# A vision transformer tower on one core: router logits four images side by side, two images loaded and scaled at the end of attention, and another order of the work in the output projection

## The reference, cut to what matters

```python
# layer 0, router: x1 is [8*1030, 192], 16 experts, each takes its capacity of best rows
scores = sigmoid(x1 @ gate_weight.T)
topk_score, topk_ids = top_k(scores.T, capacity)            # capacity 1030
out = (silu(xg @ Wg) * (xg @ Wu)) @ Wd * topk_score         # then added to its rows, and a shared expert
# layer 1, attention over 12 heads of 16; then
h3 = h2 + merge(heads) @ Wo + bo                            # the output projection
x3 = norm(h3)                                               # what router and experts of layer 1 take
logits = x3 @ w_router.T                                    # 8 experts, top 2 of each row
shared = (silu(x3 @ sg.T) * (x3 @ su.T)) @ sd.T
...
```

## Time and profile before

| | |
|---|---|
| runs before | 4337.36 to 4343.58 us, median 4338.93 |
| the profiled execution | 4339.47 us, of which the profile's span is 4337.6 |
| PE busy | 3865.1 us, 89% of the span |
| DVE, ACT, POOL busy | 2486.9, 1475.4, 1315.0 us |
| PE weight loads (PEld) | 2323.4 us |
| data moved | 353.99 MB, mean 82 GB/s |

### The profile page before, as it was taken

The page is one execution under the profiler, slowest core; times in us unless marked ns, Lnnn a source line. Parts: engine busy times, 40 slices in busy tenths (PEclk is TensorE's granted clock), DMA queues, the critical chain, the costliest instruction groups (busy, mean ns, idle before and its releaser), DMA issues. The chain is left out here.

```text
span 4337.6 us, 74538 instructions
## 1 busy us (share of the span) xinstructions
PE 3865.1 (89%) x23745; PEld 2323.4 (54%) x23747; DVE 2486.9 (57%) x4680; ACT 1475.4 (34%) x2946; POOL 1315.0 (30%) x1533
## 2 busy tenths in 40 slices
PE   8899778799999998666999999999996878799998
PEld 8788545466666666333233333333332555577776
DVE  1566468522222222787887787778783547644444
ACT  0222114211111111343577777777774111111111
POOL 0222004244444443555000001000001112177776
PEclk9999999899999999776899999999998989999999
DMA  6221111333333331245433333333215532277775
GB/s 225 66 64 53 33 41 40 105 64 63 63 63 63 62 62 19 87 143 147 60 46 46 46 46 53 51 57 46 46 27 125 144 89 42 77 163 172 173 172 121
DMA packets 336725, 353.99 MB, mean 82 GB/s; under 512 B 53036, under 2 KB 298083, under 8 KB 335023
## 3 DMA queue, kind: packets, MB, share of 16 engines
q1 hardware_dynamic: 251999, 268.42, 25.7%
q0 software_dynamic: 62272, 62.25, 9.3%
q10 hardware_dynamic: 22288, 20.93, 1.6%
HBM read 241.18 MB, written 110.47 MB: 81 GB/s over the span
## 5 line engine op out<-in xcount | busy, mean ns | idle before, releaser
L2170 DVE TENSOR_REDUCE at_mx<-psum 128x1 f32<-128x998 f32 (+1 forms) x768 | 885.3, 1190 | 231.8 <-PE psum L1983 231.3
L2125 ACT ACTIVATE at_p<-psum 128x512 f32<-128x512 f32 (+3 forms) x1536 | 851.6, 588 | 301.7 <-PE psum L2057 271.6
L2057 PE MATMUL psum<-at_q,at_k 99*128 99x512 bf16 (+3 forms) x1536 | 522.8, 383 | 20.1 <-issue 15.1
L1983 PE MATMUL psum<-at_k,at_q 96*128 96x512 bf16 (+3 forms) x1536 | 476.1, 393 | 48.9 <-DVE at_mxl L2177 19.8
L2043 PE MATMUL psum<-at_p,at_v 128*32 128x486 f32 (+3 forms) x3072 | 408.1, 603 | 1.0 <-ACT at_p L2125 0.7
L1256 ACT ACTIVATE ex_silu<-psum 128x384 f32<-128x384 f32 (+1 forms) x288 | 131.5, 457 | 768.6 <-PE psum L1200 638.3
L1287 DVE TENSOR_TENSOR ex_hT<-ex_silu,psum 128x384 f32<-128x384 f32 (+1 forms) x288 | 147.6, 512 | 416.1 <-ACT ex_silu L1256 270.6
L2057 PEld LDWEIGHTS psum<-at_q,at_k 99*128 99x128 bf16 (+1 forms) x1536 | 155.7, 102 | 426.3 <-ACT at_p L2125 271.7
L1949 POOL DMA_DIRECT2D recips<-at_shares x24 | 12.8, 533 | 1042.1 <-DVE at_mx L2170 726.4
L1222 PE MATMUL psum<-ex_wd,ex_hT 128*128 128x192 f32 (+1 forms) x1728 | 291.5, 327 | 0.0
L1222 PEld LDWEIGHTS psum<-ex_wd,ex_hT 128*128 128x128 f32 (+1 forms) x1728 | 264.2, 179 | 15.8 <-issue 3.6
(11 more groups left out here) (397 smaller groups left out, 7051.5 us busy)
## 6 DMA issues: line engine op xcount, KB each, us to landing
mx_wd<-in_e_dT SPq DMA_DIRECT2D x72, 288.0 KB
qk_parts<-hd_parts SPq DMA_DIRECT2D x32, 579.4 KB
at_k<-qk_parts SPq DMA_DIRECT2D x144, 128.8 KB, 5.1
at_q<-qk_parts SPq DMA_DIRECT2D x144, 124.8 KB, 4.8
tok_p<-in_x SPq DMA_DIRECT2D x12, 1176.0 KB, 12.9
mx_wg<-in_e_gT SPq DMA_DIRECT2D x72, 192.0 KB
mx_wu<-in_e_uT SPq DMA_DIRECT2D x72, 192.0 KB
v_rows<-hd_v_out SPq DMA_DIRECT2D x8, 1536.0 KB
```

Of the source, the lines that this page charges most:

```text
L1983: mm = pe.matmul(psum[0:ctx_rows[t], 3 + 2 * ((PRO + n) % 2) + k, 0:w], Q[v][0:R6, j * 1024 + 128 * t:j * 1024 + 128 * t + ctx_rows[t]], K ...
L2057: pe.matmul(psum[0:n, i % RING, 0:w], K[u][:, j, 128 * t:128 * t + n], Q[u][:, j * 1024 + at:j * 1024 + at + w], start=True, stop=True).th ...
L2125: act.activation(P[0:n, c % 2, j, 0:w], psum[0:n, i % RING, 0:w], ACT.Exp).then_inc(exp_ready, 1)
L2170: dve.tensor_reduce(mx[0:ctx_rows[t], j * CT + t:j * CT + t + 1], pair(n)[0:ctx_rows[t], 0:CTX], AX_X, ALU.max).then_inc(s_free, 1)
```

## The change

1. Route. `gpad` holds the weights twice only (`odd` = 0 and 1, 32 columns each). The logits of image 2g+odd go to the partitions 32g + 16 odd and on: for each stretch s, 16 matmuls with 32 output partitions, in the order odd, k, g, where the four g write four different groups of 32 partitions. DVE makes 4 copies in place of 16, and POOL clears 128 numbers a partition instead of 2048.
2. Experts. The nine first gathers signal three semaphores by threes; PE turns each three when they have landed, and DVE takes the scores after the rows. The later gathers are counted from there with the same meaning.
3. Memory only: heads uses the two image buffers for its rows, attend's latent values lie where heads' cosines were, dispatch's masks lie on an image buffer. No instruction but for their addresses changes.
4. Attend's end. SP loads images 0 and 1 (before: 0); DVE also clears image 1's padding, adds the bias row and scales both images; PE makes the shift products ahead of the last values. The stores of the last quad, and the inversion of its sums, move to the start of project.
5. Project. The prologue no longer prepares image 1. `pair(0)` (the loads of images 2 and 3) stands ahead of the waits for the last quad's stores. In the prologue `scale(1, 0)` stands at its end and `norm(1)` has moved into the loop, behind `mult(0, 0)`. In each pass `norm(n-1)` now stands at the start (it was the end of the pass before), `mult(i, 5)` ahead of `norm(n)`, and each `scale` ahead of the last mult of its half. ACT does the first silu of each half ahead of the x3 store.

The parts that decide an order or a cost, of the diff:

```diff
-        gpad = sb("rt_gpad", [128, 2, B, 128])
+        gpad = sb("rt_gpad", [128, 2, 2, 32])
...
-                for b in range(B):
+                for odd in range(2):
                     for k in range(2):
-                        last = pe.matmul(psum[:, s, 0:n], gpad[:, k, b, :], x1T[:, k, b, s * W4:s * W4 + n],
-                                         start=(b == 0 and k == 0), stop=(b == B - 1 and k == 1))
+                        for g in range(B // 2):
+                            last = pe.matmul(psum[32 * g:32 * g + 32, s, 0:n], gpad[:, k, odd, :],
+                                             x1T[:, k, 2 * g + odd, s * W4:s * W4 + n], start=(odd == 0 and k == 0),
+                                             stop=(odd == 1 and k == 1), skip_group_check=True)
...
-            pe.wait_ge(gathered[0], GATHER)
             for n in range(len(CUTS)):
+                pe.wait_ge(first_in[n], 48)
                 turn(pe, 0, 0, n)
...
-            sp.wait_ge(shares_ready, QUADS + 2)
-            load_project_image(sp, o_rows, recips, h2, 0, even, even_in)
+            for b in range(2):
+                sp.wait_ge(shares_ready, (b + 1) * QUADS + 2)
+                load_project_image(sp, o_rows, recips, h2, b, images[b], images_in[b])
...
-            for u in range(3):
+            for u in range(2):
...
-            store_shares(NG - 1)
+            store_quad_shares(pool, recips, NG - 2, sent)
...
-            dve.wait_ge(even_in, PROJECT_LOAD)
-            scale_image(dve, even, scaled)
-            shares_of(NG)
+            dve.wait_ge(shift_full, 1)
+            dve.tensor_tensor(wo_g[64:65, :, 1, :], psum[64:65, 5:7, 0:D], project["bias"][64:65], ALU.add) \
+                .then_inc(bias_ready, 1)
+            for half in range(2):
+                dve.wait_ge(images_in[half], PROJECT_LOAD)
+                scale_image(dve, images[half], scaled[half])
...
+            store_quad(pool, o_rows, B - 1, QUADS - 1, sent)
+            store_quad_shares(pool, recips, B * QUADS - 1, sent)
...
-                scale(n, 1 - n)
-                norm(n, 0, n)
+                if n == 0:
+                    norm(0, 0, 0)
+                    invert_sums(dve, B * QUADS, sent)
+            scale(1, 0)
...
                 mult(i, 0)
+                norm(n - 1, i, 1)
                 take_job(n, i + 1, 0, 0)
...
+                scale(i + 1, 1)
                 mult(i, 3)
...
                 mult(i, 4)
                 rstd_of(n)
-                scale(i + 1, 1)
+
+                mult(i, 5)
                 norm(n, i + 1, 0)
-
-                mult(i, 5)
                 take_job(n + 1, i + 1, 1, 0)
...
+                if following:
+                    scale(i + 2, 0)
                 mult(i, 8)
...
-                if following:
-                    scale(i + 2, 0)
-                norm(n + 1, i + 1, 1)
```

More of the change, by code:

```diff
@@ L907, in _ @@
             dve.wait_ge(consts_in, ROUTE_CONSTS)
-            for b in range(B):
-                dve.tensor_copy(gpad[:, 0, b, b * E0:(b + 1) * E0], gate[:, 0, :])
-                last = dve.tensor_copy(gpad[64:128, 1, b, b * E0:(b + 1) * E0], gate[64:128, 1, :])
+            for odd in range(2):
+                dve.tensor_copy(gpad[:, 0, odd, odd * E0:(odd + 1) * E0], gate[:, 0, :])
+                last = dve.tensor_copy(gpad[64:128, 1, odd, odd * E0:(odd + 1) * E0], gate[64:128, 1, :])
             last.then_inc(gpad_ready, 1)
@@ L1133, in gather @@
                                             bass.IndirectOffsetOnAxis(ap=idx[0:n, half, t:t + 1], axis=0)) \
-                        .then_inc(gathered[half], 16)
+                        .then_inc(gathered[half] if turned else first_in[t // 3], 16)
             def scatter(e, half):
@@ L1802, with phase_attend @@
 PROJECT_CONSTS = 16 * 10
-def phase_attend(nc, psum, inp, qk_parts, v_rows, o_rows, recips, ident, ident_in, first, loaded0, v_loaded0,
-                 leaving, project, project_in, h2, even, even_in, prepared, sent):
+def phase_attend(nc, psum, inp, qk_parts, v_rows, o_rows, recips, ident, ident_in, heads, first, loaded0, v_loaded0,
+                 leaving, project, project_in, h2, images, images_in, prepared, sent):
     CT = 8
@@ L2104, in _ @@
             mm.then_inc(shift_full, 1)
+            values(2, B - 1, NG - 1, NB - 1)
         @block.scalar
@@ L2183, in rows_out @@
                 dve.tensor_copy(MT[:], bank.bitcast(BF16)[0:3 * NM, 0:128]).then_inc(s_free, 1)
-            def shares_of(g):
-                dve.wait_ge(sums_in, g * STORE)
-                if not isinstance(g, int) or g:
-                    dve.wait_ge(shares_stored, (g - 1) * 16)
-                dve.reciprocal(shares[:], sums[:]).then_inc(shares_ready, 1)
             def quad(g, base, ahead):
@@ L2394, in shared_out @@
                         .then_inc(y_stored, 16)
-            load(1, 1)
             def pair(i):
@@ L3512, in build @@
         project = project_consts(ctx, nc)
-        even, even_in = project_images(ctx, nc, 0), sem("pr_loaded0")
+        images, images_in = [project_images(ctx, nc, half) for half in range(2)], [sem(f"pr_loaded{half}") for half in range(2)]
         ahead, sent = project_ahead(ctx, nc), attend_leaving(ctx, nc)
@@ L3519, in build @@
             phase_heads(nc, psum, inp, y, qk_parts, v_rows, ident, ident_in, heads, heads_in, first, loaded, v_loaded,
-                        leaving)
-            phase_attend(nc, psum, inp, qk_parts, v_rows, o_rows, recips, ident, ident_in, first, loaded, v_loaded,
-                         leaving, project, project_in, y, even, even_in, ahead, sent)
+                        leaving, images)
+            phase_attend(nc, psum, inp, qk_parts, v_rows, o_rows, recips, ident, ident_in, heads, first, loaded, v_loaded,
+                         leaving, project, project_in, y, images, images_in, ahead, sent)
         slots, slots_out = sb("slot_rows", [128, NSL], I32)[:], sb("slot_rows_out", [128, NSL], I32)[:]
```

131 lines of the change are left out of this document (66 added, 65 removed).

## The result

The changed kernel takes 4276.76 us (median of 4, 4272.58 to 4282.67) where the kernel before takes 4341.26 (4 runs, 4337.36 to 4347.76): a ratio of 0.9851, 95% interval 0.9839 to 0.9863, 64.5 us less. The forecast was 4266 in a range of 4254 to 4289.

What follows compares the result with a forecast made beforehand. Project was taken as bound by its chains, no engine full, so DVE's and ACT's order counts. Route −22.9, experts −4.5, attend's end −8.2, prologue −11.3, loop −26 sum to −72.9: from 4339.5 to 4266 us, range 4254 to 4289.

Steps and rivals of the forecast that it cites:

- Route: Route's start: shorter clear, fewer copies and logits on four groups side by side save 22.9 us, bounds 15.6 to 24.
- rival (a): Route: the four column groups don't run side by side, or weight loads lie open; total 4276 to 4285; chance 0.15.
- Experts: First expert: six turns done while the last gathers come, so up(0) starts at 835.3, 4.5 us sooner.
- Attend's end: Attend to project: POOL's drain is over before PE ends, so project starts 8.2 us sooner (5 if shift product late).
- Rival (e): Attend's end: the drain isn't tied to transfers and costs 8 us wherever it stands; total 4274; chance 0.04.
- Prologue: Project's start to up(0): h3(0) lands sooner and norm(1) leaves, saving 11.3 us; bounds 2.6 to 12.3.
- rival (b): Project's prologue: h3(0) takes as long to land as before, 8.7 us less gained, total 4275; chance 0.12.
- Loop: Project's loop: new order of DVE and ACT removes PE's waits, saving 26 us; bounds 16 to 30.
- PE's own work between is 9.2: Loop's first halves, unit 0 to unit 2: PE's work is 9.2 us, against 15.85 in pass 1 before, saving 6.65.
- my 8.35: Loop's second halves, unit 5 to unit 7: PE's own work is 8.35 us; 16.0 saved over three passes.
- Rival (c): Loop doesn't gain, PE's shares bound by something unseen such as PSUM banks; total 4279 (half) or 4292 (all); chance 0.10.
- Rival (d): Project: image loads become the bound and the kernel gets slower, if a load takes more than 30 us; chance 0.02.

Runs made afterwards that it cites:

- the held load: Changed kernel, but SP begins image 2's load only when h3(0) has landed: 4280.04 us, ratio 0.9846 to the kernel before.
- the added products: Changed kernel with 12 never-read products of 412 columns on PE between jobs 2 and later of image 1 in project's prologue: 4279.58 us, ratio 0.9851 to before.

## Why the prediction was right, point by point

The direction, the range and the five places were right. The forecast gained 8 us too much: 5.2 in the prologue, 3.4 in the loop and 1.3 in attend's body, against 1.9 too little in route and at the boundary. Part of its closeness is luck: the second halves of the loop came out right by chance, as told below. No run undoes the earlier loads and scales of image 1 alone, so what they gave in the prologue is read from the timelines.

**Route** (−22.9, measured −24.6): the mechanism was right, and rival (a) falls. The size was off, by a little more than my bound of −24, because I priced a set by the earlier trace rows at 0.89 us. In the rows above, four loads and four products follow each other every 0.345 us at full clock, a set of eight in 0.69. The 1.02 us of the earlier trace rows are a group that stands alone: at the rate of the stream (0.345 us for 412 columns) its two passes of 486 columns are 0.81, and the other 0.2 are not paid again by each set of a stream. One record of 412 columns took 0.35 in the old form ((30.11 − 2) us over 32,960 columns, times 412), so four groups cost what one did. The clock was 0.50 for the first four us, about as the forecast had it (the loads lie 0.69 us apart until 462.2, 4.8 us in).

By the rule of the Trainium skill that I weighed ("TensorE: Matmul & The Clock Gate", Part 3: Packing small matmuls), that weight loads overlap products in flight only where the row group differs, this would be 10 us more. The trace disagrees for this form: four loads one after another at the 105 ns of the earlier trace rows are 0.42 us, more than the 0.345 in which loads and products together pass. The trace before could have settled what I left open: each load takes 105 ns or more, but the eight of the group in the earlier trace rows were busy for 0.16 us together, not for 0.84:

```profile
3298.10 0.16 PEld L2043 LDWEIGHTS psum<-at_p,at_v 128*32 128x32 f32 x8 [0.22 <-issue]
```

**Experts** (−4.5): right to the tenth; three turns remain behind the last gather, 809.08 to 810.71.

**Attend's end** (−8.2, measured −8.4): right. The drain was the length of the old gap, it came with a transfer of POOL's right ahead of the block's end (why it lasts 8 us stays open), and moving the stores over the boundary cost nothing. Rival (e) falls, since the drain lay hidden. What I left at nothing, attend's body, varied by 1.3 us with experts; that is within the scatter between executions (904 to 916 us for experts alone), and the new addresses of the change's third point were not tried apart.

**Prologue** (−11.3, measured −6.1): two failed steps. "With image 1 already there I take 8.2 us to land": take_job came at 19.8 us from the start, not 17.8. I named image 2's load under rival (b) and took it as no difference; the held load shows it to be these 2 us: with it gone take_job is where I had it (17.4), bounded by norm and inversion.

The second: "From T1 to up(0) ... I take 15.0": it took 18.2. I took the norm out of it and forgot what stood before it: PE used to run image 1's late first jobs just ahead of T1, and at jobs 2 to 4 the granted clock was 0.93 to 1.00; now these jobs are done early and PE stands still for 8 us, with a clock of 0.50 to 0.56 behind it. 2.5 us of the 3.2 are that: jobs 2 to 4 took 6.12 us where they took 3.63, and 3.53 behind the added products. The other 0.7 is the norm I took off: up(0) waited for POOL's copies (`pr_xr`), the norm ended 1.3 us after up(0) (3361.71), and with it back in its place nothing changed. It was never on the path.

**Loop** (−26, measured −22.6): the order is the cause (21.3 when undone). The three kinds of term came out as −10.1 (first halves, forecast −12.05), −16.1 (second halves, −16.0) and +3.6 (the rest, +2.1). Second halves as forecast: unit 5 to unit 7 takes 8.3 us three times, for 14.3, 13.3 and 13.4. First halves: "PE's own work between is 9.2" failed. Pass 0 takes 11.4 (forecast 11.0), pass 1 11.8 (forecast 9.2), pass 2 10.2 (forecast 11.3). I had put silu 0 ahead of the x3 store and let "norm and store lie beside unit 1", but in ACT's list silu 1 stands behind that store. PE's own work between is less than 9.2: with the stores later it is 7.65 in passes 1 and 2, and the wait for silu 1 was what I left out. With the stores later, 15 us more are gained, 37.5 under before, where my bound for the loop was 30.

The rest of the loop is where the scales now stand: unit 2 to unit 5 takes 20.5, 22.1 and 22.2 us for 19.9, 19.9 and 20.3, 4.7 more in all, and unit 7 to the next unit 0 (or dispatch) 1.1 less. The scale ahead of mult 3 costs 0.2 to 0.5 us a pass between units 3 and 5 (forecast 0.7). But in passes 1 and 2, 1.7 more lie between units 2 and 3: unit 2 comes behind the waits of 4.02 and 2.35 us for `pr_hT`, and the clock was 0.57 in the 4 us from 3387 and from 3445. The second halves' 8.3 us still hold 1.7 of waiting each, so my 8.35, meant as PE's own work alone, came out right by chance: with the stores later it is 6.9 in the first pass. Rival (c) held in this weak form: a list of ACT's bound the loop, not the PSUM banks. Rival (d) never came near.

## What to carry to other kernels

When an operation is moved out of the way of a chain, ask for the next link of the same chain too: it freed silu 0 and left silu 1 behind the same transfer, and half a fix cost 15 us. An engine that computes for a loop should issue its stores where its own gap is, after the last result that PE waits for. And before a phase's end, look which engine issued the last transfer: a drain of 8 us can be moved under work by giving that transfer to the next phase.

## What was not expected of the hardware

- Four products with 32 output columns each, on four groups of 32 output partitions and from different images, passed in 0.345 us, the time of one of 412 columns. Their weights needed no time of their own.
- POOL's sequencer took 7.3 to 8.3 us to drain at the end of attend after one transfer as after nine, though the last one landed 1.6 to 1.8 us after its issue.
- The issue of three transfers of one x3 store took 1.6 us in most places and 4.27 us where SP was issuing its loads at the same time (the earlier trace rows has 2.21, the unedited kernel run again 3.55); the same in a gap took 1.76. That SP's issues are the cause was not tried apart.
- The same code, from the first expert's products to PE's first in heads, took 904 to 916 us in different executions. It goes with the group of runs: counted to heads' first operation on POOL, it was 895.8 to 897.0 us in the four traces of the first group, 900.7 to 904.4 in the four of the second and 901.6 to 902.1 in the three of the third. Each group ran on another chip; whether the chip makes it so stays open.
